# A two-layer transformer kernel: another order of its steps and another choice of their PSUM tiles

## What is computed

```python
x = _layernorm(x + _L0_attn_ref(x, ...))
x = _layernorm(x + _L0_ffn_ref(x, w1, w2, w3))
x = _layernorm(x + _L1_attn_ref(x, ...))
x = _layernorm(x + _L1_ffn_ref(x, ...))
```

## Time and profile before

| | |
|---|---|
| median of 3 runs | 442.24 us (442.02 to 443.8) |
| the profiled execution | 439.05 us |
| its span, first to last instruction | 437.2 us |
| TensorE (PE) busy | 351.0 us, 80% of the span |
| VectorE (DVE) busy | 308.1 us, 70% |
| ScalarE (ACT) busy | 221.8 us, 51% |
| GpSimd (POOL) busy | 178.2 us, 41% |
| mean granted TensorE clock | 0.948 of full speed |

### The profile page before, as it was taken

The page is one execution under the profiler, slowest core; times in us unless marked ns, Lnnn a source line. Parts: engine busy times, 40 slices in busy tenths (PEclk is TensorE's granted clock), DMA queues, the critical chain, the costliest instruction groups (busy, mean ns, idle before and its releaser), DMA issues.

```text
span 437.2 us, 8262 instructions
## 1 busy us (share of the span) xinstructions
PE 351.0 (80%) x2700; PEld 199.5 (46%) x2700; DVE 308.1 (70%) x807; ACT 221.8 (51%) x464; POOL 178.2 (41%) x216
## 2 busy tenths in 40 slices
...
GB/s 235 320 265 224 225 222 247 42 41 50 0 2 49 0 1 2 54 165 94 49 1 1 0 3 27 72 74 100 26 1 74 62 75 123 92 151 73 85 132 62
DMA packets 25981, 38.53 MB, mean 88 GB/s; under 512 B 2258, under 2 KB 21266, under 8 KB 25938
## 3 DMA queue, kind: packets, MB, share of 16 engines
...
## 4 chain that ended last, share of the span: by engine, by line
PE 43%; DVE 19%; issue 7%; ACT 6%; POOL 2%; SPq 2%; DMA 1%; POOLq 0%; DVEq 0%; ACTq 0%
DVE arena_mixers L1334 7%; PE psum_a L616 6%; PE psum_a L894 5%; PE psum_a L863 5%; PE psum_a L908 5%; PE psum_a L753 4%; PE psum_b L825 2%; PE psum_b L616 2%; ACT arena_mixers L1064 2%; PE psum_b L765 2%; PE psum_a L815 2%; PE psum_b L901 1%; SPq L553 1%; DVE cut_weights L1170 1%; PE psum_b L882 1%
## 5 line engine op out<-in xcount | busy, mean ns | idle before, releaser
L1548 POOL TENSOR_TENSOR ln_rstd<-ln_var_eps,minus_half 128x1 f32<-128x1 f32 x32 | 22.7, 709 | 78.0 <-DVE ln_var_eps L1161 78.0
L616 PE MATMUL psum_a<-cut_weights,x_transposed 128*128 128x512 f16 (+1 forms) x210 | 38.6, 334 | 13.8 <-DVE cut_weights L1170 12.6
L1334 DVE TENSOR_REDUCE arena_mixers<-psum_a 128x2 f16<-128x768 f32 (+3 forms) x44 | 47.0, 1124 | 0.9 <-PE psum_a L799 0.7
L1064 ACT ACTIVATE arena_mixers<-psum_a 128x1024 f32<-128x1024 f32 (+2 forms) x48 | 40.6, 885 | 7.9 <-PE psum_a L815 7.6
L1537 POOL DMA_INDIRECT expert_out<-block_out,arena_ffn x30 | 29.6, 988 | 31.2 <-ACT block_out L1115 27.5
L1565 POOL TENSOR_SCALAR_AFFINE_SELECT arena_mixers<-arena_mixers 128x256 f32<-128x256 f32 (+1 forms) x48 | 24.1, 513 | 34.6 <-ACT arena_mixers L1064 34.4
L894 PE MATMUL psum_a<-cut_weights,stage 128*128 x180 | 32.0, 314 | 6.1 <-issue 5.5
L863 PE MATMUL psum_a<-x_transposed,cut_weights 128*128 128x512 f16 (+1 forms) x144 | 34.8, 394 | 0.7 <-issue 0.3
L616 PEld LDWEIGHTS psum_a<-cut_weights,x_transposed 128*128 128x128 f16 x210 | 19.9, 104 | 29.4 <-DVE cut_weights L1170 13.2
L1553 POOL TENSOR_TENSOR arena_ffn<-arena_ffn 128x512 f16<-128x512 f32 (+1 forms) x12 | 14.0, 1178 | 41.6 <-ACT arena_ffn L1034 41.6
L825 PE MATMUL psum_b<-arena_mixers 128*32 128x512 f32 (+3 forms) x256 | 24.2, 457 | 6.9 <-POOL arena_mixers L1565 5.3
...
## 6 DMA issues: line engine op xcount, KB each, us to landing
expert_in<-in_row_init SPq DMA_DIRECT2D x1, 10140.0 KB, 51.1
...
stage<-in_wsh SPq DMA_DIRECT2D x5, 437.0 KB, 10.7
...
```

The lines of the kernel that those rows point to most:

```text
L616: ins = mm(dst, lhs[k][a], rhs(k, b, col), start=(k == 0 and a == 0 and b == 0), stop=(bias_at is None and k == n - 1 and a == 1))
L1064: ins = nc.scalar.activation(heads, by_row_tile(ps, se_heads(j))[:, :, :, 0:w], ACT.Exp, scale=1.0 / 16)
L1334: v.tensor_reduce(ST[:, i, 0, h0:h0 + n_h, 48].rearrange("p (h s) -> p s h", s=2), by_row_tile(ps, n_h)[:, :, :, 0:(i + 1) * P], AX.X, ALU ...
L1548: g_.tensor_tensor(rstd[:, r:r + 1], veps[:, r:r + 1], half[:, 0:1], ALU.pow).then_inc(ln_rstd[layer], 1)
```

## The change

Only the text ORDER is replaced. The set of steps, their instructions, the buffers, SyncE's program and the dependences stay; of 599 steps 570 move by fewer than five places, and 142 of 447 choices of a PSUM tile differ. Cut to the lines that hold the start, the block loads and the tail:

```diff
@@ -95,38 +95,36 @@
...
 ORDER = """
-    cen split bias cen split cen split split proj:a1 rot split pg:a0 pg:a2 proj:a1 tqk:b1 wsum proj:a1 split split
-    split sc:a1 sc:a2 wsum rot kv:b0 proj:a0 ret:b0 tqk:b1 rot vr:a0 proj:a1 tqk:b1 sc:a0 sc:a2 rx:b0 kv:b1 kv:b0
-    wsum sc:a2 rot yg tqk:a1 yh ret:b0 sc:a0 sc:a1 rot vr:b1 wo0:b1 gsum:a1 proj:a2 quant ln0 rx:b1 sc:a1 tqk:a0
-    ret:b0 sc:a0 vr:b0 yg quant proj:a1 tx0:a0 yh ret:b1 vr:a2 quant rx:b0 yg rot proj:a0 rx:b1 yg kv:a1 tqk:a0
-    rot kv:b1 yh sc:a0 sc:a1 sc:a0 wo0:a2 split tqk:a0 ret:a2 wo0:b0 bias yh vr:b1 ln0 wo0:b0 rot kv:a0
-    ret:b1 rx:b0 sc:a1 tqk:b1 sc:a0 sc:a2 yg ln0 ln0 yh tx0:a1 tx0:b0 split sc:a0 tx0:a2 vr:b1 wo0:b0 ln0
...
-    rt:b1 rc su:a2 pv se:a1 se:a0 pv:b0 sh se:a0 pv se:a2 rk:b1 rk:a0 su:a1 sx sx rb:b1 pv se:a0 se:a2 sh sh pv
-    se:a0 se:a1 su:a2 su:a1 pv:b0 se:a2 pv se:a0 bx:b1 bx:a1 sh bx:a2 bi bi pv pv ya:b1 ya:b0 su:a1 bu:a0 sh
-    bx:b0 bu:a2 ty:b1 bu:a0 bt:a2 bx:b1 wo2:b0 bu:a0 bx:a1 sh bx:b0 ty:b1 ya:a0 ya:a1 ln2 bt:b0 bd:a2 bu:a0 bx:a2
-    wo2:b0 tx2:b1 bi ln2 bt:a0 bu:a2 ty:b1 sd:a1 rt:a0 bx:b1 sd:a2 tx2:a1 bt:a0 ty:b1 wo2:b0 bd:a1 rt:b0
...
-    bx:b0 bu:a2 bt:a1 bu:a0 bx:b0 bt:b1 bx:a2 bu:a1 bd:a0 bt:b1 bx:b0 bi bu:a2 os os bd:a0 bt:b0 bx:b1 bu:a1 fin
-    bd:a0 bd:a2 bx:b1 bt:b0 bd:a0 bu:a2 bx:b1 bt:a0 fin bu:a1 bt:a2 bx:b0 bu:a0 bx:b1 ln3 bd:a1 bt:b0 bd:a2
-    bd:a0 os os bu:a2 bt:b1 bu:a0 bt:b1 fin bx:b0 bu:a1 ln3 ln3 bd:a0 bt:b1 bd:a2 bx:b0 bd:a0 sh bu:a2 bu:a1 bt:b1
-    bd:a2 bt:b0 bd:a0 bt:b1 bd:a2 bd:a1 fin ln3 sd:a0 sd:a2 sd:b1 sd:a0 os os fin os fin os ln3 fin ln3 fin ln3
-    ln3
+    cen bias split cen split cen split split proj:a0 rot pg:a2 pg:a0 proj:a1 tqk:b0 split wsum rot proj:a1 split
+    split sc:a1 sc:a2 kv:b0 split wsum proj:a0 ret:a2 tqk:b1 rot vr:a0 proj:a2 tqk:b1 rx:b0 sc:a0 sc:a2 kv:a1 wsum
+    kv:b1 sc:a0 ret:b1 rot rot tqk:b0 yg yh sc:a0 sc:a2 vr:b1 wo0:b1 gsum:a1 quant ln0 proj:a2 sc:a1 tqk:a0 ret:b0
+    sc:a2 rx:b0 vr:b1 yg quant proj:a1 ret:b0 kv:b1 yh vr:a0 quant rx:a2 yg rot proj:a0 rx:b1 yg tqk:a0 rot kv:b1
+    sc:a0 sc:a1 wo0:a2 sc:a0 yh yh split tqk:a1 tx0:b1 bias ret:a2 wo0:b0 vr:a1 ln0 wo0:b0 rot ret:b1 sc:a1 kv:b0
+    rx:a0 tqk:b1 sc:a1 sc:a0 yg ln0 ln0 sc:a2 yh tx0:b1 tx0:b0 tx0:a2 vr:b1 wo0:b0 ret:a0 rx:b0 ln0 vr:b1 up:a1
+    split split cut up:a0 up:a2 cut cut rx:b0 up:a0 yg yg yh cut up:a2 tx0:b0 up:a1 cut cut wo0:b1 ret:a1 dn:b0 ln1
...
+    se:a0 sx rt:b1 rc su:a2 rk:b1 pv se:a0 se:a1 sh pv:b0 se:a1 pv se:a0 rk:a0 su:a2 sx sx pv pv se:a0 se:a1 rb:b0
+    se:a0 sh sh se:a1 su:a2 su:a1 sh bx:b1 pv:b0 se:a0 pv se:a2 bx:b1 bi bx:a0 pv pv ya:b1 bu:a2 ya:b0 bi su:a1
+    bx:b0 ty:b1 sh bu:a0 bu:a2 sh wo2:b0 bx:b1 bt:a2 bu:a0 bx:b1 bx:b0 ya:a0 ty:b1 ln2 ya:a1 bt:b0 bu:a0 bx:b1 bd:a2
+    bi tx2:a2 wo2:b0 bt:a0 bu:a2 bx:b1 ln2 bt:a0 ty:b0 sd:a1 rt:a0 sd:a2 ty:b1 tx2:a1 wo2:a0 bd:a1 rt:b1 rc rc bt:b1
...
+    bt:a1 bt:b1 bx:b0 bu:a2 bx:a1 bd:a0 bi bt:b0 bu:a2 bx:b1 os os os bd:a1 bd:a0 bt:b0 fin bx:b1 bu:a1 bt:b0 bd:a2
+    bd:a0 bu:a2 bt:b1 bx:a0 bx:b0 bu:a1 ln3 bt:a2 bx:b1 bu:a0 bd:a1 bd:a2 bx:b1 fin bt:a1 bd:a0 bu:a2 sh os bt:b1
+    bx:b0 bu:a1 bt:b1 fin bu:a2 bx:b0 bd:a0 bd:a1 bt:b1 ln3 ln3 bd:a0 bu:a2 bt:b1 bu:a1 bt:b0 bd:a0 bt:b1 bd:a2
+    bd:a1 bd:a0 fin ln3 sd:a2 sd:b0 sd:b1 sd:b1 os os os os fin fin ln3 fin ln3 fin ln3 ln3
 """
```

More of the change, by code:

```diff
@@ new lines @@
+    sc:a0 sc:a1 wo0:a2 sc:a0 yh yh split tqk:a1 tx0:b1 bias ret:a2 wo0:b0 vr:a1 ln0 wo0:b0 rot ret:b1 sc:a1 kv:b0
+    rx:a0 tqk:b1 sc:a1 sc:a0 yg ln0 ln0 sc:a2 yh tx0:b1 tx0:b0 tx0:a2 vr:b1 wo0:b0 ret:a0 rx:b0 ln0 vr:b1 up:a1
+    split split cut up:a0 up:a2 cut cut rx:b0 up:a0 yg yg yh cut up:a2 tx0:b0 up:a1 cut cut wo0:b1 ret:a1 dn:b0 ln1
+    vr:a0 dn:b1 dn:b0 ln1 rx:b0 tx1:a1 tx1:b1 ln1 yg yh dn:a2 yh ln0 tx1:a1 ln1 wo0:a0 wo0:b0 qk:a1 tx0:a0 ln0 ln0
+    split tx1:b1 qk:a2 qk:a0 tq:a2 qk:a0 mx:a1 mx:a0 tq:a1 tq:a0 mx:a1 mx:a0 tq:a1 mx:a2 mx:a1 mx:a0 tm:b0 mx:a1
```

17 lines of the change are left out of this document (13 added, 4 removed).

## The result

The changed kernel takes 454.34 us (median, 452.36 to 459.39) where the kernel before took 442.24 us (439.22 to 444.94) beside it: a ratio of 1.033, with an interval of 1.027 to 1.040. It is slower by 3.3%, and the prediction of 439.3, with a range to 444.0, is wrong in sign. Run again on another chip it took 452.14 against 439.58, a ratio of 1.029 (1.021 to 1.038).

The account below looks back on a forecast made before the run. The prediction saw no engine bounding the whole kernel, so each stage was judged by its own. Terms 0 + 0 - 2.5 - 1.0 + 0.6 = -2.9 took the profiled 439.05 to 436.15, plus 3.19 for a 439.3 median; range 435.0 to 444.0.

Parts of the forecast that it names:

- Terms a and b: Front: bias 0 earlier gains 1.2 us, split 4 later delays loads; together taken at 0, bounds -1.2 and +4.3.
- Much is made up: Front: most of the up to +4.3 us from ScalarE's stall at split 8 is recovered elsewhere.
- the third rival: Slower: the first wsh piece holds up split 8, nothing is made up, +4.3 us, 443.6 in all; chance 0.18.
- The 2.25 gap: TensorE's 2.25 us wait at 81.45 for y_transposed on VectorE, claimed to go because yh 3 now precedes split 8.
- The 8.9 idle us: TensorE's idle time from 75 to 125 us, in which the remaining 0.35 us of the stall could vanish.
- Start a: Kernel start: bias 0 ahead of split 0 lets TensorE's first matmul come 1.2 us earlier.
- Term c: Attention of layer 1, 216 to 250 us: VectorE has the same list reordered; taken at 0, bounds -1.9 and +1.9.
- Term d: Block loads after rb 0: bi 5 later lets queued VectorE work fill its 4.24 us wait; -2.5, bounds 0 and -5.3.
- the rival "no change": Block loads: TensorE waits 2.3 us at bx 0 with pv queued behind, cancelling the 2.5 gain; 441.8, chance 0.30.
- the larger rival: Rb 0 escapes GpSimd's pair, 2.8 us more, and the start's 1.2 survives: 435.3; chance 0.16.
- Term e: Expert blocks of the tail, 386 to 417 us: TensorE's gaps of 0.52 and 0.72 mostly go; -1.0, bounds -2.0 and +1.0.
- Term f: Last two sd, both on tile B1: the last waits for VectorE's read; +0.6 us, bounds 0 and +0.6.

Follow-up runs that it names:

- experiment 5: The kernel before with its first 92 steps in the changed order, but split 4 back ahead of pg 0: 441.29 us, ratio 0.998 to the kernel before.
- experiment 6: The changed kernel with split 4 back ahead of pg 0 and steps 249 to 320 as before: 444.52 us, ratio 1.009 to the kernel before.
- experiment 1: The changed kernel with split 4 alone moved back ahead of pg 0: 449.17 us, ratio 1.012 to the kernel before.
- experiment 8: The kernel before with steps 341 to 450 alone (the block loads) as changed: 441.49 us, ratio 1.003 to the kernel before.
- experiment 10: The changed kernel with split 4 back ahead of pg 0, steps 249 to 320 and the last 149 as before: 438.81 us, ratio 0.999.

## Why the prediction was wrong

**Terms a and b, "Much is made up": the first step that failed.** The chain of events was read rightly, if a little too small: row_init 5.36 later (said 3.2 to 4.4), the wsh piece at 79.5 (said 77.9 to 79.1), ScalarE standing at split 8 with TensorE behind. This was the third rival, at 0.18, turning the sum to a loss "from 2.9 carried". What failed is the credit set against it. The gains lie *ahead* of the wait: wo 0 2 began on TensorE at 73.59 where it began at 77.51 before. They bring ScalarE earlier to a load whose time is fixed by SyncE, and so they lengthen the wait, to 6.15, instead of paying for it. The 2.25 gap was no credit: wo 0 3, which had it, stands on TensorE behind vr 4, as it did before, and the input of vr 4 is made by ScalarE behind split 8; so wo 0 3 came at 83.94, later than the 81.45 of before. The 8.9 idle us of the stage were no reserve either, since TensorE, idle for 8.44, then ran at the lower clock for 5 us more. Up to wo 0 3 a and b together cost 2.46 in the table, where the sum had 0; by the times at the end split 4's late place alone costs some 6.5. The Trainium skill ("DMA: Bandwidth & Descriptors", section "Queues, rings and completion order") says that each engine consumes its ring in order; by that rule, the prediction said, the front would cost the whole 4.3, which it then talked down. The trace agrees with the page again, with the piece 1.05 behind row_init. Start a itself was right: TensorE's first matmul came at 10.73 (said 10.8, before 12.04), and the front without the stall gains 2.3. But in experiment 5 no gain is left at the end.

**Term c, attention taken at 0 with bounds of 1.9 either way.** It measured +1.95 against the profile before (1.84 over the same steps), and no profile with the changed order there comes below 35.85, none with the old one above 33.90; experiment 6, which undoes it with the attention's last steps ahead of it, loses 2.5 less than experiment 1. The prediction argued from VectorE's list of work, which is the same; its bad bound mirrored the good one and came from no row. What changed is who waits for whom, for about half of it between two maxima on one tile, and the prediction set no price on any of the 142 changed tiles but sd 7's.

**Term d, the block loads: right in mechanism, and too small in its place.** VectorE's timeline around the load table, GpSimd's sh pair, and TensorE at bx 0 and bx 3:

```profile
291.82 0.50 DVE L1402 TENSOR_TENSOR arena_ffn<-arena_ffn 128x120 f32<-128x120 f32 x1
...
293.03 1.17 DVE L1406 SCALAR_TENSOR_TENSOR arena_ffn<-arena_ffn 128x15 uint32<-128x15 f32 x1
...
294.32 1.00 DVE L1408 TENSOR_SCALAR arena_ffn<-arena_ffn 128x15 uint32<-128x15 f32 x1
...
308.22 0.16 DVE L1431 TENSOR_TENSOR arena_ffn<-arena_ffn 128x5 f32<-128x5 f32 x1
```

```profile
293.01 2.28 POOL L1530 TENSOR_TENSOR arena_ffn<-arena_ffn 128x512 f16<-128x512 f32 x2
```

```profile
299.01 0.38 PE L880 MATMUL psum_b<-constants,arena_ffn 128*128 128x128 f32 x2
...
309.59 0.44 PE L880 MATMUL psum_b<-constants,arena_ffn 128*128 128x128 f32 x2
```

Bi 5 starts without a wait (4.24 before), bx 0 without one too, so the rival "no change" did not come about. L1404 (now L1402) took 0.50 where it took 3.22; it escaped the pair, as the larger rival wanted, but a later instruction met it (1.17), so the rows that the loads wait for came 1.75 earlier and not 2.8 (3.97 us from rb 0's start to the end of L1406, 5.72 before). The 1.00 of L1408 stands behind them. From the end of bx 0 to the end of bu 2 TensorE took 12.6 to 12.8 us, where the old stretch took 16.35, 19.17 and 18.41: some -3.7, against -2.5. But by bt 6 it had given 1.3 of this back, by bd 14 1.9 more, and experiment 8 shows that nothing is left at the end. That last loss, from bt 6 to bd 14, was not tried apart and stays open; so does that from qk 0 0 to mx 1 0 0, which experiment 10 still has (93.1).

**Term e, the tail, taken at -1.0 with bounds of -2.0 and +1.0: failed in sign.** It measured +3.38. The low clock, 3.40 us long, can account for at most half of its length, 1.7; in the profiles with the clock at 1.00 the order alone cost 0.5 to 1.7. "Four steps, not two, ahead of the gather additions" counted steps of a list in which bt, bu and bx give GpSimd nothing to do: on GpSimd bi 25 stood no farther from the additions than before, and three of them came at once, so that it took 3.54 us where it took 2.73. The other longer gaps on TensorE had no row in the prediction, and neither had the clock: the premise that "every term is idle time" leaves out instructions that run longer.

**Term f, the two sd on b1: right.** TensorE's timeline near its end:

```profile
436.51 2.23 PE L614 MATMUL psum_b<-cut_weights,arena_ffn 128*128 128x256 f16 x18 [0.67 <-DVE residual L1422]
```

0.67, said 0.6.

One slip in the prediction changes nothing: -5.3 for d with the other terms as taken gives 436.5, which is inside the range down to 435.0 and not 1.5 us short of it.
